# The setup of a gated cross-attention and ffn kernel, put in another order

## What is computed

```python
x = x + tanh(g_xattn[0]) * xattn0(layernorm(x), ctx)   # relu projections q, k, v; relu scores; relu output
x = x + tanh(g_ffn[0])   * ffn0(layernorm(x), k0, k1, k2, s0, s1, s2)
x = x + tanh(g_xattn[1]) * xattn1(layernorm(x), ctx)   # argmax gather, 16 heads
x = x + tanh(g_ffn[1])   * moe1(layernorm(x))          # shared expert and the 8 best of 64 experts

def ffn0(x, k0, k1, k2, s0, s1, s2):                   # k0 512x1024, k1 1024x1024, k2 1024x256, all bool
    dense = lambda kb, h: h @ where(kb, 1.0, -1.0)
    h = s0 * dense(k0, concatenate([x, -x]))
    h = s1 * dense(k1, relu(h) * 2)
    return s2 * dense(k2, relu(h) * 2)
```

## Time and profile before

| what | us |
|---|---|
| three timed runs: median, lowest, highest | 1814.24, 1812.26, 1815.61 |
| the profiled execution, from its first to its last instruction | 1871.9 |
| TensorE busy in it (matmuls) | 1702.8 |
| VectorE busy | 1322.4 |
| ScalarE busy | 985.6 |
| GpSimd busy | 945.8 |
| TensorE's first matmul after the setup's transposes | at 22.43 |
| start of the first ffn layer | at 38.76 |

### The profile page before, as it was taken

How to read it: one execution, slowest core, us unless ns; L and a number is a source line. 1 busy time by engine, 2 the same in 40 slices (tenths; PEclk the granted TensorE clock), 3 DMA queues, 4 the chain that set the end, 5 groups by cost and what they waited for, 6 DMA issues and landing times.

```text
span 1871.9 us, 51471 instructions
## 1 busy us (share of the span) xinstructions
PE 1702.8 (91%) x17308; PEld 1435.5 (77%) x17308; DVE 1322.4 (71%) x4639; ACT 985.6 (53%) x2819; POOL 945.8 (51%) x1507
## 2 busy tenths in 40 slices
PE   3799999999999999999999999999999997448785
PEld 2688888888888888888888888888888876347675
DVE  5467777777777777777777777777777775436554
ACT  2355555555555555555555555555555554224443
POOL 2114555555555555555555555555555554345555
PEclk8899999999999999999999999999999999579998
DMA  7401111111000001000000000000000012138886
GB/s 219 145 9 50 44 40 38 41 41 35 25 24 22 31 14 31 30 21 24 23 25 24 27 19 20 20 22 17 23 23 20 21 45 73 47 91 209 193 199 138
DMA packets 102656, 101.12 MB, mean 54 GB/s; under 512 B 38879, under 2 KB 92073, under 8 KB 102616
## 3 DMA queue, kind: packets, MB, share of 16 engines
q1 hardware_dynamic: 68824, 81.43, 14.0%
q0 software_dynamic: 33792, 19.17, 5.9%
HBM read 51.63 MB, written 111.84 MB: 87 GB/s over the span
## 4 chain that ended last, share of the span: by engine, by line
PE 45%; issue 17%; DVE 14%; POOL 8%; DMA 8%; ACT 7%; SPq 1%; POOLq 0%; DVEq 0%; ACTq 0%
PE bank L1085 13%; PE bank L990 8%; DMA out<-ey,aid 7%; POOL table L615 5%; PE ps_lg L1143 3%; ACT p L802 3%; PE ps_yo L1099 3%; PE ps_yo L990 3%; PE bank L1071 3%; PE ps_tr L1016 3%; PE ps_m L990 2%; PE ps_pt L1158 2%; ACT xr L741 2%; DVE pt_l L1634 2%; DVE rmax L1629 2%
## 5 line engine op out<-in xcount | busy, mean ns | idle before, releaser
L615 POOL DMA_INDIRECT table<-xs,slot x496 | 504.0, 1016 | 201.5 <-issue 171.9
L802 ACT ACTIVATE p<-ps_lg,rmax 128x77 f32<-128x77 f32 x1024 | 235.6, 349 | 144.5 <-DVE rmax L1629 139.4
L1085 PE MATMUL bank<-h_h,held 128*128 128x256 f16 x2048 | 266.8, 273 | 4.1 <-issue 2.0
L557 POOL TENSOR_TENSOR pool_pad<-pad_in 128x1 f32<-128x1 f32 x352 | 67.9, 193 | 397.1 <-PE ps_lg L1143 176.8
L1085 PE MATMUL bank<-h_l,held 128*128 128x256 f16 x2048 | 266.8, 274 | 0.0
L1085 PEld LDWEIGHTS bank<-h_l,held 128*128 128x128 f16 x2048 | 201.0, 98 | 24.4 <-issue 0.6
L1085 PEld LDWEIGHTS bank<-h_h,held 128*128 128x128 f16 x2048 | 195.6, 98 | 28.4 <-DVE h_l L1564 2.6
L631 POOL TENSOR_TENSOR rs<-nt,minushalf 128x2 f32<-128x2 f32 x128 | 92.9, 726 | 200.2 <-DVE nt L1529 188.7
L1564 DVE SCALAR_TENSOR_TENSOR h_l<-bank,h_h 128x512 f16<-128x512 f32 x256 | 175.0, 684 | 11.6 <-ACT h_h L783 6.9
L1629 DVE TENSOR_REDUCE rmax<-ps_lg 128x8 f32<-128x616 f32 x128 | 101.8, 795 | 85.7 <-PE ps_lg L1143 84.7
L706 POOL DMA_INDIRECT out<-ey,aid x64 | 98.7, 1542 | 99.0 <-DVE aid L1902 65.0
(11 more groups left out here) (277 smaller groups left out, 4604.0 us busy)
## 6 DMA issues: line engine op xcount, KB each, us to landing
ew<-in_e_wts SPq DMA_DIRECT2D x48, 384.0 KB
table<-xg SPq DMA_DIRECT2D x8, 1284.0 KB, 16.0
xg<-table SPq DMA_DIRECT2D x64, 160.5 KB
xs<-xr SPq DMA_DIRECT2D x31, 320.0 KB, 2.6
x<-in_x SPq DMA_DIRECT2D x32, 256.0 KB
out<-x SPq DMA_DIRECT2D x32, 256.0 KB
table<-xs,slot POOLq DMA_INDIRECT x496
held<-in_e_wts SPq DMA_DIRECT2D x16, 384.0 KB, 4.4
```

The lines of the kernel that those rows point to most:

```text
L615: g.indirect_dma_start(out=table, out_offset=bass.IndirectOffsetOnAxis(ap=slots[:, t, k:k + 1], axis=0), in_=rows[:, t, :], in_offset=None ...
L802: ins = a.activation(p32[:, h * S2:(h + 1) * S2], ps_lg[:, h // HB, h % HB * S2:(h % HB + 1) * S2], ACT.Exp, bias=rmax[r % 2][:, h:h + 1])
L1085: ins = mm(two(bank[j % 2])[:, m % 2, :], wb1[:, k, m * P:(m + 1) * P], hp[:, k, :], start=(i == 0 and k == 0), stop=(i == 1 and k == FK - 1))
```

## The change

The instructions stay the same but for one that is split in two. What changes is their order and the place of some waits, all of it ahead of or inside the first batches:

- ScalarE takes the high half of batch 0's turned rows ahead of the tanh of the gates.
- VectorE takes the low half of them ahead of `fold_gates` and of k0.
- VectorE's `body(-1)` is written out, with k1 in two halves in it: the first half between `a_l` and `a_x1`, the second between `ln_shift(1, 0)` and the low half of x1's turned rows. k2 stays behind the body.
- TensorE's one wait for all three weights becomes a wait for k0 at the first layer of batch 0, for k1 at the second and for k2 at the third.
- SP loads ctx and x of batch 1 ahead of the wait for k1, and so ahead of sgu_w.

```diff
@@ -436,10 +436,10 @@
 
             sp.wait_ge(bools_ok, 1)
             load_split(9)
+            load_ctx(1)
+            load_x(1)
             sp.wait_ge(bools_ok, 2)
             load_split(8)
-            load_ctx(1)
-            load_x(1)
             for k in range(0, E, E // 8):
                 clear_table(range(k, k + E // 8))
             load_ctx(2)
@@ -729,8 +729,6 @@
                         a.activation(hi, landed, ACT.Copy, scale=WS).then_inc(setup_hi, 1)
 
             split_high(FOR_A)
-            act.wait_ge(small_dma, 16 * 9)
-            a.activation(tg[:, :], raw[:, 0:4], ACT.Tanh).then_inc(gates_tanh, 1)
             act.wait_ge(consts2, 31)
 
             def ln_norm(i, b, src, dst):
@@ -930,7 +928,10 @@
                 d_ac(2, b)
                 d_ac(3, b)
 
-            body(-1)
+            first(-1)
+            act.wait_ge(small_dma, 16 * 9)
+            a.activation(tg[:, :], raw[:, 0:4], ACT.Tanh).then_inc(gates_tanh, 1)
+            second(-1)
             split_high(FOR_C)
             body(0)
             split_high(FOR_D)
@@ -1061,6 +1062,8 @@
             def b_l0(j, b):
                 if j == 0:
                     pe.wait_ge(tr_lo[1], b + 1)
+                    if isinstance(b, int) and b == 0:
+                        pe.wait_ge(bools_ok, 1)
                     w(pe, gu_ac.sem, gu_ac.nth(2, b - 2))
                 elif j == 1:
                     w(pe, gu_ac.sem, gu_ac.nth(3, b - 2))
@@ -1074,6 +1077,8 @@
             def b_l1(m, b):
 
                 j = m // 2
+                if m == 0 and isinstance(b, int) and b == 0:
+                    pe.wait_ge(bools_ok, 2)
                 if m % 2 == 0:
                     if j < 2:
                         pe.wait_ge(l0_lo.sem, l0_lo.nth(j + 2, b))
@@ -1090,6 +1095,8 @@
             def b_l2(t, b):
 
                 if t == 0:
+                    if isinstance(b, int) and b == 0:
+                        pe.wait_ge(bools_ok, 3)
                     pe.wait_ge(l1_lo.sem, l1_lo.nth(2, b))
                     w(pe, pt_lo_ok.sem, pt_lo_ok.nth(7, b - 1))
                 for k in range(FK):
@@ -1369,7 +1376,6 @@
             pe.wait_ge(consts2, 31)
             pe.wait_ge(setup_lo, 5)
             body(-1)
-            pe.wait_ge(bools_ok, 3)
             body(0)
             pe.wait_ge(setup_lo, 10)
             body(1)
@@ -1491,7 +1497,7 @@
                 do(v.tensor_copy(sc[:, 7:8], tg[:, 3:4]))
                 setup.wait()
 
-            def from_bools(k):
+            def from_bools(k, half=1):
 
                 dve.wait_ge(bools_in[k], 16)
                 if k == 0:
@@ -1500,7 +1506,10 @@
                     ins = v.tensor_scalar(wb0[:, :, :], wb0[:, :, :], sg[:, 0:1], None, ALU.mult)
                     setup.end()
                 elif k == 1:
-                    ins = v.tensor_scalar(wb1[:, :, :], byte_rows(1), 0.5, sc[:, 6:7], ALU.subtract, ALU.mult)
+                    fk = slice(half * FK // 2, (half + 1) * FK // 2)
+                    ins = v.tensor_scalar(wb1[:, fk, :], byte_rows(1)[:, fk, :], 0.5, sc[:, 6:7], ALU.subtract, ALU.mult)
+                    if half == 0:
+                        return
                 else:
                     ins = v.tensor_scalar(wb2[:, :, :], byte_rows(2), 2.0, 1.0, ALU.mult, ALU.subtract)
                 ins.then_inc(bools_ok, 1)
@@ -1864,11 +1873,19 @@
 
             ln_first(0)
             split_low(FOR_A)
+            dve.wait_ge(consts2, 31)
+            tr_low(0, 0, xt_l[0], xt_h[0])
             fold_gates()
             from_bools(0)
-            from_bools(1)
-            dve.wait_ge(consts2, 31)
-            body(-1)
+            a_v(0)
+            a_l(0)
+            from_bools(1, 0)
+            a_x1(0)
+            ln_sums(1, 0, x1, x1_ok)
+            ln_moments(1)
+            ln_shift(1, 0)
+            from_bools(1, 1)
+            tr_low(1, 0, xt_l[1], xt_h[1])
             from_bools(2)
             split_low(FOR_C)
             body(0)
```

## The result

| what | before | changed |
|---|---|---|
| timed runs on one chip, four of each: median, us | 1813.78 | 1803.68 |
| lowest and highest, us | 1812.26, 1815.61 | 1800.24, 1806.45 |
| ratio, with its 95% interval | | 0.9939 (0.9921 to 0.9957) |
| profiled execution, span, us | 1871.9 | 1798.5 |

The forecast was 1804.0. The medians lie 10.1 us apart; the ratio, applied to 1813.78, says 11.1, from 7.8 to 14.3. The two spans must not be subtracted from each other: kernels ran on several chips, on which the kernel before takes 1814, 1862 or 1880 us. The span of 1871.9 is like that of a slower one; the span of 1798.5 belongs to one of the timed runs, 1800.24.

What follows compares the result with a forecast made beforehand. It took latency ahead of TensorE's first dense work as the bound: 9.73 - 0.4 - 0.15 + 1.14 = 10.3 us, taken as 10.2 for the long profile, giving 1804.0 us. The range was 1800.6 to 1808.5.

Steps and rivals of the forecast that it cites:

- The reading: Start of the kernel: latency before TensorE's first dense work bounds the gain, and the loop carries it whole to the end.
- Part 1: Batch 0's xt_h and xt_l made first: q projection starts at 12.70 in place of 22.43, -9.73 us.
- Part 2, first half: First half of k1 between l and x1 takes 2.3 us and makes x1 start 0.4 us late.
- Rival (a): Byte conversion in k1 slower than its size says, 4.6 us a half: gain 6.0, 1808.2 us; chance 6%.
- Part 2, second half: Second half of k1 behind nb, ending between 27.3 and 27.8 if GpSimd holds it; taken as +0.15 us.
- Part 3: First ffn layer waits for k0 alone, k2 behind its xt_l: -1.14 us, first h_l just hidden.
- Part 4: SP's queue: sgu_w and the clears issued later or earlier, sgu_w landing by 63.3, needed at 65.3: cost 0.
- Rival (c): Gain caught by something that does not move, sgu_w landing behind the clears: up to 1814 us; chance 7%.
- The clock: TensorE's granted clock may rise or fall earlier or later; one low stretch costs 1.6 us, added on each side.
- Rival (b): Clock rises earlier, first layer at full clock: 3.0 us more gain, 1801.0 us; chance 4%.
- (d): Clock stays low through batch 0's second and third layers: 15.0 us lost, net +4.7, 1818.9 us; chance 3%.
- The 57.7 us: Profiled 1871.9 us against timed median 1814.24; if evenly long, gain 10.0 in place of 10.3; 10.2 was taken.

Runs made afterwards that it cites:

- e1: The changed kernel with TensorE's single wait for all three ffn weights put back ahead of the first batch's body; 1803.33 us, ratio 0.9941 to the kernel before.
- e5: The changed kernel with SP's old order, sgu_w ahead of ctx and x of batch 1; 1803.44 us, ratio 0.9939 to the kernel before.
- r2: The kernel before, unchanged, run again on another chip; 1879.51 us, ratio 0.999.
- e10: The changed kernel with k1 in four pieces and the shared expert's split inside batch 0, VectorE's part behind the second h_l; 1859.5 us, ratio 0.9885.
- e9: The kernel before with only batch 0's turned rows moved first, k1 whole behind k0, one wait; 1874.03 us, ratio 0.9967.
- the first group: Follow-up runs on one chip, where the kernel before took 1862.22 us.
- the four of the second: Follow-up runs on another chip, where the kernel before took 1815.24 us.
- r1: The changed kernel itself, run again; 1803.37 us, ratio 0.994 to the kernel before.
- e7: The changed kernel with the split of the shared expert's weights moved into batch 0's body; 1843.15 us, ratio 0.99 to the kernel before.

## Why the prediction was right, step by step

**The reading** held: a chain of waits at the start, no gap in the loop to catch a gain. The time was 1803.68 for 1804.0. Some of the terms were off, with both signs. The figures here are those of the first profile of the kernel before, on which the sum was made.

- **Part 1**: -9.36 for -9.73. xt_h 0.63 to 0.70 ahead of xt_l and 0.75 to TensorE were as read. The transposes began 0.22 later in this execution (10.43 for 10.21), which has to do with the loads, and xt_h followed them by 0.09 instead of a few hundredths. The idle time of TensorE is 1.55 for the 1.4 forecast. In two executions of the changed kernel the q projection started at 13.07 and 13.43, in e1 at 12.77: a spread of 0.7 that the sum did not have.
- **Part 2, first half**: it takes 2.26 to 2.34 and starts 7.10 after the q projection, not 7.0 (6.56 and the 0.42 of l), so x1 comes 0.53 after its due time and not 0.4. Of this the half accounts for 0.33 (x1 follows the end of `o` by 0.36, before by 0.03), as read; the other 0.20 is `o` itself, 9.00 behind the q projection in place of 8.80. Rival (a), 4.6 us a half, is out.
- **Part 2, second half**: taken as +0.15, measured 0 to within the 0.18 that xt_l still waits for ScalarE. Here the mechanism was named rightly and its victim wrongly. Of VectorE and GpSimd one did hold the other; but VectorE's half had begun at 25.42, `cx_l` at 25.65, and it was GpSimd's copy that took 2.38 instead of 0.32. Its waiting cost nobody anything. The SBUF — State Buffer page of the Trainium skill (Who interferes with whom) says of the exclusive lock that whoever starts first keeps it for the whole instruction. The trace agrees with it: GpSimd ends at 28.03, 0.17 behind the half. The prediction took its upper bound, 27.8, to follow from this rule of the Trainium skill, and that was a misreading by its own times, which had the half at 25.04 and the copy at 25.19 (21.95+3.24): VectorE first, and so not held.
- **Part 3**: -1.13 for -1.14 in place. k2 and the three splits behind it, computed to end 0.15 ahead of the first h_l, ended just there (the sum put xt_l at 0.61, its length in the chain at 21.77, where the row at 36.88 has 0.69; with that the room is 0.07): h_l begins at 31.34 with no idle time before it, 2.55 after TensorE, as before (2.56).
- **Part 4**: 0 for 0. The bound of 63.3 for sgu_w's landing was far from the truth, 34.3: transfers queued behind it didn't delay it by more than 1.4 us (6.4 for 5.0). Rival (c) never came near; e5 shows that the whole reordering of SP is worth nothing.
- **The clock**: the sum left it at 0 with 1.6 each way, and it took both signs. The first layer gained 0.46 (second layer less first: 8.00 before, 7.54 after); the transposes ahead of gu_h lost 0.24 (0.86 before, at a granted clock of 1.00; 1.10 after, at 0.50); the second part of batch 1's first layer lost 0.60 (1.05 for 8 matmuls before, 1.65 after); and the stretch of the earlier trace rows at 92.3 has no counterpart, which gained 1.67 (5.32 to 3.65), the 1.6 that the prediction had put on such a stretch. In sum 1.3 for the changed kernel, in these two executions. It can't be put down to the change: r2, with nothing changed, takes 7.56 where the kernel before took 8.00, and has its transposes at 1.10. Only the missing fall stands in both profiles of the changed kernel and in neither of the kernel before (5.32 and 5.21). Rival (b) would have been 3.0 and the 0.46 is no more than r2 shows without it; (d) did not happen: the second layer's 48 matmuls took 5.40 in both.
- **The 57.7 us** between the span and the timed runs, which I spread evenly or gave to nothing, are the chip's, as far as the traces tell. In the window of 400 to 1000 us TensorE has 6309 matmuls in the profile of before and 6514 in that of the changed kernel, which alone would look like a faster loop. But here is the same window (columns as in the earlier trace rows) of r2 and of e10, which ran on one chip, the one without the change and the other with it:

```profile
400.00:1000.00 600.00, 587.52 (x6271) 497.90 (x6268) 458.23 (x1607) 343.86 (x995) 327.87 (x555) 1.00 0.09 26
```

```profile
400.00:1000.00 600.00, 585.80 (x6271) 496.15 (x6271) 458.19 (x1607) 342.64 (x997) 327.05 (x558) 1.00 0.09 25
```

Both have 6271, and e9 on that chip 6291; the four kernels of the first group have 6318 to 6335, the four of the second 6503 to 6513. The loop's pace goes with the chip and not with the kernel. So the sum should have been taken whole, 10.3, rather than scaled by 1814/1872. That the difference was 0.1 was luck of size, not of method. The sum's lower bound, 9.8, doesn't quite follow: with the half held to 27.8 and the 0.3 of h_l lost, the terms give 9.9.

So the number was met a little better than its working deserved. In the traces 0.37 and 0.13 were lost in parts 1 and 2, 0.15 won in the second half and 1.3 by the clock: 11.25 in all where 10.3 stood. The ratio's 11.1 agrees with both and, with 7.8 to 14.3, doesn't tell them apart; nor do the traces, since against r2 the gain at that point is 9.4.

**A term the sum hid**: it counted 9.7 for the rows and 0.4 against k1. e9 shows that of the 9.7 only 4.9 to 5.7 belongs to the rows alone, and the rest to k1 behind v and l.

## What to carry to other kernels

At a kernel's start, read the chain backwards from the first dense work and ask of each piece who needs it; what only a later stage reads goes into the waits that are already there, cut to the size of the wait. Price such moves together: an early start is worth only a part, here about half, if the next instruction on the same engine stands behind the old block. And where VectorE's long instructions on SBUF are moved, look at what GpSimd has on the chain beside them: its smallest instruction can take as long as the whole one on VectorE.

## What the runs showed of the hardware

- **GpSimd is held by VectorE.** A copy of 128x154 took 2.38 us in place of 0.32 when it began 0.23 after a conversion of 128x4096 on VectorE, and 1.85 beside one of 128x3072; a root of 128x2 took 2.67 in place of 0.70 when it began 0.17 after gu_l (2.28). Each ended behind the instruction on VectorE, whose own length was as elsewhere or nearly so (2.28; 2.44 where the first half took 2.34).
- **Conversions of bytes** on VectorE: 0.75 for 128x1024, 1.14 to 1.37 for 2048, 1.81 to 1.91 for 3072, 2.26 to 2.44 for 4096, 4.40 to 4.49 for 8192.
- **TensorE's clock** was at 0.50 (1.2 GHz) at the start of the first layer in the kernels before and after, behind a stretch with little for TensorE, and rose within the layer. In batch 1's first layer a late rise went with no further fall in four executions and an early one with a fall at the second layer in eight of nine, a net 1.1 us, so that a change of 1 us ahead of it can be blurred or doubled: 1.19 became 0.37 and then 2.04 between r1 and e1. That the point shifts from run to run is also what TensorE: Matmul & The Clock Gate (What's actually happening) of the Trainium skill says, and the traces agree: from the first to the second layer the kernel before took 8.00 and 7.56 (r2), the changed kernel 7.54 and 7.36 (r1). The prediction's "a few us" is not what that section of the Trainium skill states; its figure is 0.5 us either way for the point of the rise.
- **Chips differ** more than most changes: the kernel before took 1814, 1862 and 1880 us on three of them. In the chain of the slower ones from 600 to 648 us, 17.1% (before) and 16.8% (e7) is time that waits for nothing the profile shows, 2.06 us of it at once ahead of a root on GpSimd; in the changed kernel's own profile TensorE's second layer leads that list with 28.2%. What sets a chip apart stays open.
